# Batch ends of self attention moved into the next batch, and cross attention's keys stored in four chunks, in a decoder layer on one core

## The reference

```python
def self_attention(x):                      # 16 heads of 8
    xn = rmsnorm(layernorm(x)) * norm_w     # the kernel's norm steps
    q, k, v = heads(xn @ Wq.T + bq), heads(xn @ Wk.T + bk), heads(xn @ Wv.T + bv)
    s = where(causal, q @ k.T / sqrt(8), -inf)
    return xn + merge(softmax(s) @ v) @ Wo.T + bo     # added to x
def cross_attention(x, y):                  # y: (8, 1601, 96)
    q = heads(layernorm(x) @ Wq + bq); k, v = split(y @ Wkv + bkv)
    return merge(softmax(q @ k.T / sqrt(8)) @ v) @ Wo + bo   # added to x
def rotary_attention_and_experts(x): ...    # 16 heads of 64; q and k rotated by position
```

## Time and profile before

| | us |
|---|---|
| median of three runs | 1686.04 |
| the profiled execution | 1688.64 |
| its span, first to last instruction | 1686.5 |
| first self attention scores | 64.2 |
| cross attention block from | 311.6 |
| rotary attention from about | 1008 |
| TensorE busy in the span | 1451.8 (86%) |
| VectorE, ScalarE, GpSimd busy | 1077.7, 919.7, 563.7 |
| mean granted TensorE clock | 0.93 |

### The profile page before, as it was taken

The page is one execution under the profiler, slowest core; times in us unless marked ns, Lnnn a source line. Parts: engine busy times, 40 slices in busy tenths (PEclk is TensorE's granted clock), DMA queues, the critical chain, the costliest instruction groups (busy, mean ns, idle before and its releaser), DMA issues. The chain is left out here.

```text
span 1686.5 us, 29040 instructions
## 1 busy us (share of the span) xinstructions
PE 1451.8 (86%) x10917; PEld 735.4 (44%) x10941; DVE 1077.7 (64%) x2029; ACT 919.7 (55%) x1996; POOL 563.7 (33%) x695
## 2 busy tenths in 40 slices
PE   1577768798989898989899897899999998899998
PEld 1344435233333333333333332566666666544443
DVE  4755543777778686868687781666566654565554
ACT  0223324376777677767778683455555555343433
POOL 4201012030303021120303000788788887233331
PEclk9977878699999899989999995999999999899999
DMA  4222225313232324242323200000000000000001
GB/s 98 62 66 49 54 61 115 67 72 58 69 66 47 99 50 103 50 103 50 103 50 94 45 2 12 1 1 1 1 1 1 1 1 1 7 21 20 21 20 35
DMA packets 76974, 75.01 MB, mean 44 GB/s; under 512 B 12196, under 2 KB 66340, under 8 KB 75940
## 3 DMA queue, kind: packets, MB, share of 16 engines
q1 hardware_dynamic: 76836, 73.16, 19.1%
HBM read 42.47 MB, written 30.16 MB: 43 GB/s over the span
## 5 line engine op out<-in xcount | busy, mean ns | idle before, releaser
L1302 DVE TENSOR_REDUCE b_chunk_max<-psum 128x2 f32<-128x800 f32 x502 | 483.6, 990 | 135.2 <-PE psum L1503 118.2
L1430 ACT ACTIVATE b_prob<-psum 128x512 f32<-128x512 f32 (+1 forms) x832 | 452.9, 595 | 148.2 <-PE psum L1543 132.8
L1543 PE MATMUL psum<-q_stack,k_stack 50*128 50x256 bf16 (+1 forms) x1664 | 288.1, 284 | 29.3 <-ACT b_prob L1430 20.9
L1503 PE MATMUL psum<-k_stack,q_stack 48*128 48x400 bf16 x1004 | 252.1, 350 | 40.4 <-DMA k_stack<-b_k_scratch 35.3
L1513 PE MATMUL psum<-b_prob,b_v_aug 128*32 128x256 f32 (+1 forms) x3328 | 281.1, 411 | 0.0
L1543 PEld LDWEIGHTS psum<-q_stack,k_stack 50*128 50x128 bf16 (+1 forms) x1664 | 103.7, 97 | 213.8 <-ACT b_prob L1430 171.1
L1703 POOL TENSOR_SCALAR c_prob<-c_prob,c_rec 128x128 f32<-128x128 f32 (+1 forms) x256 | 192.5, 771 | 9.2 <-POOL c_kT L1712 8.6
L2118 DVE TENSOR_TENSOR e_hg<-e_gl,e_gate 128x512 f32<-128x512 f32 x124 | 123.3, 1017 | 88.6 <-PE psum L2166 84.0
L1821 ACT ACTIVATE c_prob<-psum,c_mneg 128x128 f32<-128x128 f32 (+1 forms) x256 | 104.3, 419 | 136.2 <-DVE c_mneg L1763 136.2
L1786 DVE SCALAR_TENSOR_TENSOR c_turned<-psum,c_bias,c_tab 128x256 f32<-128x256 f32 x256 | 106.1, 476 | 112.2 <-PE psum L1919 112.2
L2058 ACT ACTIVATE e_gl<-psum,b1T 128x512 f32<-128x512 f32 x124 | 85.2, 687 | 127.6 <-PE psum L2161 123.8
(11 more groups left out here) (236 smaller groups left out, 1947.8 us busy)
## 6 DMA issues: line engine op xcount, KB each, us to landing
k_stack<-b_k_scratch SPq DMA_DIRECT2D x32, 600.4 KB, 10.3
b_k_scratch<-b_kparts SPq DMA_DIRECT2D x7, 1200.8 KB, 4.4
b_k_scratch<-b_kparts SPq DMA_DIRECT2D x7, 800.5 KB, 6.1
b_ctxT<-in_ctx SPq DMA_DIRECT2D x8, 600.4 KB, 12.0
e_w<-in_L_ffn_re_w SPq DMA_DIRECT2D x62, 64.0 KB, 1.9
a_scratch<-a_parts SPq DMA_DIRECT2D x16, 192.0 KB, 2.2
q_stack<-b_q_scratch SPq DMA_DIRECT2D x32, 96.0 KB, 2.2
b_k_scratch<-b_kparts SPq DMA_DIRECT2D x7, 400.2 KB, 6.8
```

The costliest lines, as they stand in the source:

```text
L1302: nc.vector.tensor_reduce(out=chunk_max[:, half, q, pair:pair + 3:2, c], in_=max_banks(v)[:, :, 0:w], axis=AX.X, op=ALU.max).then_inc(max_ ...
L1430: nc.scalar.activation(prob[0:k, buf, par * 2 * T:(par + 1) * 2 * T], st_bank(par)[0:k, :], ACT.Exp, scale=HD ** -0.5).then_inc(exp_done, 1)
L1503: last = nc.tensor.matmul(max_banks(T_.now("unit"))[:, k, 0:hi - lo], qst[rows, h, q * P:q * P + P], kst[rows, h // 2, lo:hi], start=True, ...
L1543: last = nc.tensor.matmul(st_bank(par)[0:k, (hh // 2) * T:(hh // 2) * T + T], kst[rows, h // 2, n * P:n * P + k], qst[rows, h, :], start=T ...
```

## The change

What it does, part by part:

- In self attention the values of step 7 and the last pv move to step 0 of the next batch, attnT to step 1, and out to step 2, ahead of x. m moves to step 6. The 12 maxima units are at steps 2 to 5, three in each. The program gets a ninth batch of three steps, which only ends batch 7. `a_resid` has three buffers for two.
- ScalarE issues the four DMAs of the shift rows, from inside its m item. SyncE's program has none of them left in this block, and waits for the stack's buffer with a constant.
- ScalarE makes the first bf16 part as well (four activations for the two of before), GpSimd makes the other two parts of the queries, VectorE those of the keys, in three operations of 256 columns each. The keys are stored first.
- Masks cover only the 128 columns of each head that lie on the diagonal, in a matmul after the others, for those of before that covered all of them. The maxima's matmuls name their 48 rows (`tile_position`).
- `b_v_aug` is filled in batch 2. The order of the rotary weights is made on the host, and they come in four DMAs, 2.1 MB in all, at the front of `load_weights`; the 18 DMAs of `load` for the raw weights and biases, and GpSimd's 8 copies, are gone.
- In cross attention the keys are stored chunk by chunk, 12 DMAs for 3, at the same place in SyncE's program.

The diff, cut to its core:

```diff
-        ITEMS_AT = {0: "v", 2: "x", 3: "pv", 4: "qk", 5: "pv", 7: "pv"}
-        UNITS_AT = [range(n * UNITS // STEPS, (n + 1) * UNITS // STEPS) for n in range(STEPS)]
+        UNITS_AT = [range(lo, hi) for lo, hi in ((0, 0), (0, 0), (0, 3), (3, 6), (6, 9), (9, 12), (12, 12), (12, 12))]
+        def items_of(b, n):
+            late, more, further = b >= 1, b + 1 < B, b + 2 < B
+            items = {0: [("pv", b - 1, late)], 1: [("attnT", b - 1, late)],
+                     2: [("out", b - 1, late), ("x", b + 2, further)], 3: [("pv", b, b < B)], 4: [("qk", b + 2, further)],
+                     5: [("pv", b, b < B)], 6: [("m", b + 1, more)], 7: [("pv", b, b < B)]}[n]
+            return [(kind, of) for kind, of, there in items if there] + early.ITEMS.get((b, n), [])
...
@@ SyncE
+            def bounce(b):
+                for which in (1, 0):
+                    sp.wait_ge((q_parts_ready, parts_ready)[which], b + 1)
+                    bounce_parts(sp, scratch[b % 2][which], parts[:, :, which * T:which * T + T], which, bounced)
+            def stack(b):
+                sp.wait_ge(bounced, 2 * BOUNCES * 16 * (b + 1))
+                if b >= 2:
+                    sp.wait_ge(st_full, STEPS * (b - 1))
+                for which, operand in enumerate((qsts[b % 2], ksts[b % 2])):
+                    load_stack(sp, operand, scratch[b % 2][which], which, slice(0, H // 2), stacked[b % 2])
...
@@ GpSimd
+            def split(b):
+                pool.wait_ge(qk_ready, b + 1)
+                own(nc.gpsimd.tensor_tensor(rest[:, 0:T], qk[:, 0:T], parts[:, 0, 0:T], ALU.subtract))
+                own(nc.gpsimd.tensor_tensor(parts[:, 1, 0:T], rest[:, 0:T], early.zeros[:, 0:T], ALU.add))
+                nc.gpsimd.tensor_tensor(parts[:, 2, 0:T], rest[:, 0:T], parts[:, 1, 0:T], ALU.subtract).then_inc(q_parts_ready, 1)
...
@@ ScalarE
                 elif kind == "m":
-                    act.wait_ge(prep_full, n)
                     nc.scalar.activation(mparts[:, 0, :], prep[0:H, 0:T], ACT.Copy).then_inc(m0_ready, 1)
+                    for m, ready in enumerate((m0_ready, m1_ready)):
+                        act.wait_ge(ready, b + 1)
+                        for par in range(2):
+                            nc.scalar.dma_start(stack_rows(qsts[b % 2], 0, par, SHIFT_ROW + m, 1, slice(0, H // 2)),
+                                                mparts[par * 8:par * 8 + 8, m, :]).then_inc(m_stacked, 16)
...
@@ TensorE
-                for par in range(2):
-                    nc.tensor.matmul(psum[:, 4 + 2 * (n % 2) + par, 0:2 * w], identb[:],
-                                     t["mask_kq%d" % kt][:].rearrange("p h q -> p (h q)"), start=True, stop=False)
...
+                for par in range(2):
+                    bank = psum[:, 4 + 2 * (n % 2) + par, 0:2 * w].rearrange("p (h q) -> p h q", h=2)
+                    last = nc.tensor.matmul(bank[:, :, 0:P], identb[:], t["mask_kq"][:], start=False, stop=True)
...
+            def attend(b):
+                for n in steps_of(b):
+                    units = UNITS_AT[n] if b + 1 < B else range(0)
+                    if n == 0 and b >= 1:
+                        values(b - 1, STEPS - 1)
+                    if n == 0 and b + 1 < B:
+                        item("v", b + 1, 0)
+                    if b < B:
+                        if n == 0:
+                            pe.wait_ge(m_stacked, 4 * 16 * (b + 1))
+                        scores_t(b, n)
+                    maxima(b + 1, units[:1])
+                    if n >= 1 and b < B:
+                        values(b, n - 1)
+                    maxima(b + 1, units[1:])
+                    for kind, of in items_of(b, n):
...
@@ cross attention, SyncE
-                sp.wait_ge(k_split, T_.up("kchunk", 4))
-                bounce_parts(sp, k_scr, kparts[:], 1, k_bounced)
+                for lo, hi in CHUNKS:
+                    sp.wait_ge(k_split, T_.up("kchunk"))
+                    bounce_parts(sp, k_scr[:, :, lo:hi], kparts[:, :, lo:hi], 1, k_bounced)
...
@@ RotaryTables.load_weights
+        for m, name in enumerate(("q", "k")):
+            sp.dma_start(self.w12[:, m].rearrange("p w n -> p (w n)"), a["L0_ffn_%s_w" % name]).then_inc(self.w_loaded, 16)
+            sp.dma_start(self.bias[:, m].rearrange("p w u -> p (w u)"), a["L0_ffn_%s_b" % name]).then_inc(self.w_loaded, 16)
```

More of the change, by code:

```diff
@@ L466, in self_attention, with program @@
         ones_set, stack_cleared, passed = sem("a_ones_set"), sem("a_stack_cleared"), sem("a_passed")
-        PER = {name: 2 * n for name, n in dict(
-            item=3 + 1 + G + 2, norm=2, next=1, batch=1, stack=1, m=1, qk=1, unit=UNITS, scores=STEPS, values=STEPS, group=G,
-            dve_own=NORM_LINKS + RMS_LINKS + 3 + G + 2, pool_own=QT).items()}
+        qk_ready, q_parts_ready = sem("a_qk_ready"), sem("a_q_parts_ready")
+        PER = ("item", "norm", "next", "unit", "dve_own", "pool_own", "qk", "m")
         block = ctx.enter_context(nc.Block())
-        def shown(kind, more, further):
-            return {"v": more, "x": further, "qk": further, "m": more}.get(kind, True)
-        def program(eng, tally, begin, attend):
+        def program(begin, attend):
             begin()
-            for i in range(B // 2 - 1):
-                for j in range(2):
-                    attend(i * 2 + j, j, True, True)
-            for j in range(2):
-                attend(B - 2 + j, j, j == 0, False)
+            for b in range(B + 1):
+                attend(b)
         @block.sync
@@ L839, in _, with item @@
             pe.wait_ge(wT_free, 1)
-            def item(kind):
+            def item(kind, b, g):
                 T_.up("item")
@@ L864, in item @@
                 elif kind == "attnT":
-                    pe.wait_ge(attn_ready, T_.now("batch"))
+                    pe.wait_ge(attn_ready, b + 1)
                     for q in range(QT):
@@ L1224, in split_k @@
             def split_k():
-                wait(pool, k_bounced, T_.now("dma"))
+                wait(pool, k_bounced, T_.now("kdma"))
+                T_.up("kdma", K_BOUNCED)
                 for c in range(4):
```

394 lines of the change are left out of this document (172 added, 222 removed).

## The result

The changed kernel is slower. It took 1732.06 us (median of four runs, 1728.38 to 1735.42) against 1687.45 us (1684.53 to 1688.90) for the kernel before on the same chip, a ratio of 1.0266 [1.0235, 1.0297]. The forecast was 1656.

A forecast was written before the change was run, and what follows sets the result against it. Self attention was taken as bound by waits (drain, key stack, half clock), cross attention by one key-stack hole per batch. Self attention -43.9, cross attention stores +12.6 and weights +2.0 sum to -29.3, giving 1656 us, range 1634 to 1677.

The forecast's parts named there:

- term (a): Self attention, step 7: ScalarE's four shift-row issues (2.6 us) delay the exponential, 2.0 us exposed per batch, bounds 0 and 3.4.
- term (c): Self attention: the x item follows the out item on one prep bank and waits for VectorE's addition, 1.0 us added.
- term (b): Self attention, steps 2 to 5: three maxima units each on VectorE add 2.1 us per batch, half a microsecond a step.
- hidden too: Self attention: shift rows, needed 2 us after issue, land under values and the v item; uncovered, about a microsecond would show.
- The half clock: Self attention, after the drain: TensorE's half clock from 123 to 135 goes, saving 2.6 us per batch.
- The first and the last batch, taken as a common period and as 0: Self attention: six periods gain 6.4 us each, 38.4 in all; batch 7, without maxima, gains 0.
- issue time stays inside the 7.3: Cross attention: issuing twelve key stores, 12 x 0.43 = 5.2 us, fits within their 7.3 us transfer; the stores add 1.8 per batch.
- The weights: Start of the cross block: 2.1 MB of rotary weights ahead of the first shift rows, +2 us, bounds 0 and 5.
- The issue is free: Rival, self attention: ScalarE's queue takes transfers without holding compute, clock never falls; period 22, time 1638; chance 0.15.
- Small runs cost nothing: Rival, cross attention: the 800-byte runs cost nothing, the cross part is +2 alone, time 1644; chance 0.18.
- The slower one: Rival, cross attention: key stores held at issue; gain used up from 0.93 us each; at 1.6, time 1738; chance 0.04.
- A new wait takes the old one's place: Rival, self attention: late stack at step 2, or maxima units hold TensorE; period 28, gain 21, time 1680; chance 0.15.

The follow-up runs named there:

- e1: Changed kernel with cross attention's three whole key stores put back in place of twelve chunk stores, rest of the change kept: 1698.6 us.
- e4: Changed kernel with three whole key stores in place of twelve, moved ahead of the third group's shift rows in cross attention: 1710.6 us.
- r1: The changed kernel as it is, measured a second time: ratio 1.0264 [1.0228, 1.0301] against the kernel before.
- b1: Kernel before, self attention untouched, with cross attention's keys stored chunk by chunk ahead of the third group's shift rows: 1648.6 us.
- n1: Changed kernel with self attention's shift rows left out (no issue, no wait, no shift in the exponentials): 1715.0 us, against 1731.6 for the changed kernel beside it.
- e2: Changed kernel with cross attention's twelve key stores cut by 32 partitions, giving long runs, in place of 400 columns: 1732.0 us.
- e3: Changed kernel with cross attention's twelve chunk stores moved ahead of the third group's shift rows, query stores still behind: 1656.1 us.
- s1: Changed kernel with self attention's stack loads issued only after the shift rows have landed: 25 us below the changed kernel the first time, 6 the second.
- s5: Changed kernel with stack loads waiting for the shift rows and VectorE's key split moved behind step 5's maxima: 1716.4 us.

## Why the prediction was wrong

Of the 76 us between forecast and measurement, 51 are self attention's (43.9 shorter forecast, 7.3 longer measured), and 19 cross attention's (12.6 and 2.0 longer forecast, 33.8 measured). The remaining 6 have no one place.

**The self attention period** (24.6 us forecast, 30.4 measured in batch 1, 31.2 on the mean of batches 1 to 5). The waits that were to go did go: no wait for a stack shows, and the drain is gone. What was added, point by point:
- Issue on ScalarE, term (a), forecast 2.0 exposed. Right: 1.83 and 1.41 in the two batches, behind 2.6 us of issue.
- The x item, term (c), forecast 1.0. Right: 0.73.
- Three units a step, term (b), forecast 2.1 "half a microsecond a step". The size was right, 2.25 + 0.50, the reason was not: it is one gap at the turn to step 5, where VectorE has its key split (0.43, 0.64 and 0.90 us) ahead of three reductions.
- **The shift rows, "hidden too". This step failed.** I had their landing as about a microsecond, by the weights' stretch, where nothing else was in flight. With the stack loads out at the same time it is 3.1 and then 3.9 us, and TensorE waits 1.3 and 2.1. In the kernel before they were ahead of the loads on one queue; the change gave them a queue of their own and so a competitor.
- **The half clock, 2.6 us counted as gone. This failed too, and it is the larger.** With the 0.8 us of the masks it should have taken 3.4 us off TensorE's busy time in a batch. That time rose by 0.5 instead (22.83 to 23.36): 3.9 us of the 5.8 that the period missed, and 1.8 are idle time, which should have fallen by 3.0 (8.1 removed, 5.1 added) and fell by 1.2. The mean clock only rose from 0.78 to 0.84. I counted the clock's gain as if all gaps would close, and the gain of the drain without the gaps that would replace it.

**The first and the last batch, taken as a common period and as 0.** Batch 0 came out 4.7 us longer and batch 7 7.4 longer. It is no accident of one execution: in the six executions with this self attention (changed, e1 to e4, r1) batch 0 took 32.8 to 38.0 us, against 29.8 before and 29.7 in b1, and batch 7 35.7 five times within 0.3 and 31.3 once, against 28.3 in both. In the changed kernel the clock stands at half over some 10 us at the start of batch 7; in e4, where it took 31.3, it does not. So at least 3 us are there without the half clock. Batch 6, forecast 5.5 us shorter, was 5.5 shorter here, and 2.8 to 5.5 over the six.

n1 gives the bound: without the rows the kernel gains 17 us, and its self attention is 9.7 us shorter than before, where 43.9 was forecast with the rows. So most of the forecast was not there to be had, rows or not. What holds the rest stays open: the gaps for the maxima are still there, but no run removed them alone, since moving the split made the stack late, and the two stretches of n1 show that the batch with the smaller gaps can be the slow one.

**Cross attention** (+12.6 forecast, +33.8 measured). Right: nothing starts earlier, and the stores stand behind the shift rows; the sign; that the queries behind them set the loads. **The step that failed is "issue time stays inside the 7.3".** I set issue (12 x 0.43) beside transfer (7.3 us at 335 GB/s) and took the larger. But issue took 7.42 us, since each store in the row took 0.62, and the query stores and their landing came behind the end of the issues: 3.0 us more per batch, not 1.8, and each hole grew by 3.6, inside my bound of 4. e2 shows no part of the rates of the earlier trace rows in it. Of the 33.8 us, 25.5 are holes for the key stack, 1.5 more waiting for shift rows, and 5.3 busy time (627.8 against 622.5). The last is scatter: in the repeat (r1) the busy time is 622.1, as before, the holes are 66.1 us, and the stretch is 729.8.
What the text missed altogether is what e3 found: it said that the chunks "start nothing earlier", named the place that prevents it, and did not ask what the same stores would be worth elsewhere. That is worth 76 us.

**The weights**, forecast +2: from the first product to the first scores of cross attention it is now 13.1 us (317.0 to 330.14), before 11.2 (312.6 to 323.83). Right, +1.9.

**The prologue.** The text said that it gains 3 us and gives them back at the first exponential. It gained 2.9, and TensorE goes on behind the first exponential at 67.80 us, in the kernel before at 70.31: 2.5 us are still in hand there. They are lost later in batch 0. Up to 77 us its matmuls take what they take at half clock (four of 256 columns 1.03 us at 68.81, 0.60 at 78.46), in the kernel before up to 67. The granted clock of the rows does not show this: it reads 1.00 from 60 to 86 us in the changed kernel.

**The rivals.** "The issue is free" is out: the exponential waited 2.70 us behind the issues. "Small runs cost nothing" was right on the runs as far as e2 can tell, and wrong on the price, since the number of issues cost instead. The slower one was priced at 1738 (by its own terms it is 1686 - 43.9 + 2 + 98 = 1742) and had 0.04. The time came out near it, by another way: the issues took 0.62 us each, below its own point of 0.93, and it was self attention's gain that failed, for which that rival had left 43.9 us standing. "A new wait takes the old one's place" had the right mechanism and too small a size, a period of 28 for 30.4. The fault common to both is that I let the cases go wrong one at a time: a new wait in self attention and dearer issues in cross attention together, with self attention's gain at nothing, give 1686 + 33.8 = 1720, and no case held them.

## What to carry to other kernels

Cutting a transfer into parts pays only if the parts can leave as they become ready; behind something that waits for the last part, it only adds issues, here 0.62 us each and 33 us in all. So put the issue where its data is made, in the same queue order as the work, and keep large transfers from standing directly ahead of small ones that an engine waits for. And when a change closes a gap, ask which engine's work is next in line there: the gap's length may come back under another name, and a share of the gain put down to the clock is the least certain of all; here it did not come.

## What the runs showed of the hardware that I had not expected

- Small transfers beside large ones. Four shift-row transfers landed within 1.2 us of the end of their issue with no stack loads beside them (s1), 3.1 and 3.9 us with stack loads in flight from another queue (changed kernel). Behind 2.4 MB of stores on the same queue even their issue took 4.37 us in place of 2.37 (e4). The Trainium skill says that queues of different engines share the same DMA engines (DMA: Bandwidth & Descriptors, Issuing engines are not separate DMA queues); these rows agree.
- A 0.29 us cast took 5.41 us beside GpSimd's 5.64 us clearing of a tile (s5). The Trainium skill has it that VectorE and GpSimd lock a shared pair of ports for whole instructions (SBUF — State Buffer, SBUF: two separate sides); the pair of rows agrees.
- A hole can cost more than its length. In cross attention 53.5 us less of waiting went with 18.4 us less of busy time for the same matmuls (0.92 to 0.98), and 30.6 less with 11.5 less between before and b1. It is no fixed rate: e4 is idle 64.2 us there, less than the 73.9 of before, and busy 640.3, more than the 622.5. In self attention two stretches of one execution with the same program stood at 0.94 and 0.57 (n1).
- Self attention of the same code took 253.0 to 265.1 us over six profiled executions, while the runs of one whole kernel on one chip lie within 3 to 24 us (e1, e4). The first result of s1, with an interval of half a per cent to each side, did not come back on another chip.
